# A four-layer cross-attention and expert network in two interleaved streams: a new order of the work on every engine, and one attention's mask added by VectorE

## The chip, the cores and the metric

The kernel runs on one core of a Trainium2 chip. The core has five engines that run their own instruction lists in order and wait for one another through semaphores: TensorE (PE, with its weight loads shown apart as PEld), VectorE (DVE), ScalarE (ACT), GpSimd (POOL) and SyncE (SP), which here only issues DMAs. The metric is the time on the device in microseconds (us) of one execution; lower is better.

## The reference, cut to what matters

Eight sequences of 256 rows of 128 numbers pass through four layers. Each layer adds a gated cross-attention over a fixed context and then a gated expert network:

```python
for n in range(4):
    x = x + tanh(g_xattn[n]) * attention_n(layernorm(x), ctx)
    x = x + tanh(g_ffn[n]) * experts_n(layernorm(x))

# attentions 0, 1, 2: 16 heads of 8, head by head
scores = q @ k.T * 8 ** -0.5      # 1: + adj and where(mask1 == 0, -inf)  2: where(mask0 == 0, -inf)
out = softmax(scores) @ v         # 1 and 2: then @ Wo + bo
# attention 3: one head of 64
# experts_0: gate and 8 SELU experts, best 2 weighted; experts_1: two quantised linear maps with a GELU
# experts_2: 8 experts of silu(x W1) * (x W3) W2; experts_3: 16 small experts on each of 8 heads
```

## The kernel before

The batch is cut into four turns `i` of two sequences (512 rows). Two turns run as two streams, one attention of one turn beside the expert layer of the other. `steps` writes the pairs out: step 1 is attention (0,0) alone; step 2 is attention (1,0) beside experts (0,0); 3 is (0,1) beside (1,0); 4 is (1,1) beside (0,1); 5 is (0,2) beside (1,1); 6 is (1,2) beside (0,2); 7 and 8 are the one-head attentions (0,3) and (1,3) beside experts (1,2) and (0,3); 9 is (2,0) beside (1,3); steps 10 to 16 repeat 2 to 8 with turns 2 and 3, and step 17 is experts (3,3) alone. So steps 2, 3, 10 and 11 hold a SELU layer, 4, 5, 12 and 13 the quantised ("bit") layer, 6, 7, 14 and 15 the SiLU layer, 8, 9, 16 and 17 the head experts.

Within a step, each engine's list is made by `play`: the attention and the expert layer are Python generators that `yield` a due time before each piece, and the piece with the smaller due time comes first in the list. Due times are unitless plans that decide order alone; in the run an engine takes its list in order and waits where a semaphore says so. No piece of a step comes ahead of one of the step before on the same engine.

An attention is an opening and then 36 slots. The opening: keys and values are projected on TensorE from the transposed context `cT`; VectorE normalises `x` (`statistics`, a power of -0.5 on GpSimd in `root`, `normal`); TensorE transposes it (`norm_T`) and projects the queries; VectorE splits the queries into three bf16 parts `qp` and SyncE stacks them into `qS` with 12 DMAs, while GpSimd splits the keys into `kp` and stacks them into `kS` with 12 more (`keys`). A slot is one pair of PSUM banks out of two pairs: "max" slots make scores that VectorE reduces to row maxima (L1205), "shift" slots turn the maxima round, "exp" slots make the scores again with the maxima taken off, ScalarE applies Exp (L965), and TensorE multiplies the result by the values (L587). "back" slots bring the heads back. The slots' due times start at 25 and lie 1.3 apart (`FIRST_SLOT`, `SLOT`); the SELU layer's 36 pieces of one matrix each lie 2.2 apart, the SiLU layer's 16 lie 4.2 apart. Beside expert layers 2 and 3, exp slots come in groups of four with one due time. The masks: for attention 1, GpSimd makes `b1q` (added to the max scores on TensorE through an identity, L538) and `bfull` (added to the exp scores by VectorE, `add_bias`, L1221). For attention 2, `l2_bias_k` is added to the exp scores on TensorE, L565, two matmuls a slot.

## Time and profile before

| | before |
|---|---|
| median of 3 runs | 1927.77 us (1922.35 to 1931.37) |
| the profiled execution | 1916.38 us, its span 1914.6 us |
| TensorE busy, weight loads | 1348.0 us (70%), 666.6 us |
| VectorE, ScalarE, GpSimd busy | 987.2 us (52%), 751.5 us (39%), 402.5 us (21%) |
| granted TensorE clock, mean | 0.841 of full |

The span is the stretch from the first to the last instruction of the program; the profiled execution's own time holds 1.8 us more. Engines are busy in parallel, so the shares don't add up to the span. In the windows views a row is a stretch of the span: its bounds and length, the busy us of PE, PEld, DVE, ACT and POOL with the number of instructions, the granted TensorE clock, the DMA engines' busy share and GB/s. In a timeline row the two numbers are start and length, and the brackets hold the idle time of the engine just before with what ended it. SPq is a DMA issue on SyncE. "issue" is idle time whose end the profile puts down to nothing; a wait for a DMA's landing is often shown so.

### The profile page before, as it was taken

What the parts mean: (1) busy time and instruction counts of PE and PEld (TensorE: products, weight loads), DVE (VectorE), ACT (ScalarE), POOL (GpSimd) and SP (SyncE); (2) the same over time, 40 slices, a digit from 0 to 9 for tenths busy, and PEclk for the clock granted to TensorE, in tenths of its full rate; (3) what the DMA queues carried; (4) which work ended last, traced back from release to release, by engine and by line L of the source; (5) the groups of instructions that cost most, each with busy time, mean ns of one, the idle gap of its engine ahead of it and who ended that gap; (6) DMA issues with size and microseconds to landing.
All of it is one profiled execution on the core that took longest, in us unless ns stands there. A gap on an engine that the chain in (4) does not pass through costs nothing.

```text
span 1914.6 us, 21114 instructions
## 1 busy us (share of the span) xinstructions
PE 1348.0 (70%) x7836; PEld 666.6 (35%) x7836; DVE 987.2 (52%) x2268; ACT 751.5 (39%) x1102; POOL 402.5 (21%) x462
## 2 busy tenths in 40 slices
PE   3456978865647697867477797886473869886756
PEld 2223544441212334531222455444121233453211
DVE  3347546656563453462552664666656445346252
ACT  0034643522324143337266463353232413433636
POOL 4306020025030200015332601001503020001424
PEclk9988999987559898969578898999755989896969
DMA  8204112112020200012420311300202020001221
GB/s 269 37 7 77 51 48 63 34 39 40 1 33 2 34 1 1 1 28 88 66 73 23 83 45 38 74 23 12 45 1 33 1 33 2 1 1 17 94 61 61
DMA packets 49221, 78.57 MB, mean 41 GB/s; under 512 B 15056, under 2 KB 34272, under 8 KB 48496
## 3 DMA queue, kind: packets, MB, share of 16 engines
q0 software_dynamic: 18752, 34.69, 7.7%
q1 hardware_dynamic: 25616, 25.25, 6.3%
q10 hardware_dynamic: 4752, 17.30, 2.9%
q8 instruction: 62, 1.02, 0.2%
q14 instruction: 39, 0.32, 0.1%
HBM read 52.63 MB, written 2.10 MB: 29 GB/s over the span
## 4 chain that ended last, share of the span: by engine, by line
PE 53%; DVE 18%; issue 12%; ACT 9%; DMA 4%; POOL 3%; SPq 1%; POOLq 0%; ACTq 0%; DVEq 0%
PE ps L705 5%; PE ps L587 5%; PE ps L721 5%; PE ps L538 5%; DVE nm L1205 4%; PE ps L809 4%; PE ps L863 3%; PE ps L543 3%; PE ps L811 3%; PE ps L852 3%; PE ps L799 3%; ACT hT L1075 3%; DVE ps L1221 2%; PE ps L570 2%; DVE hT L1403 1%
## 5 line engine op out<-in xcount | busy, mean ns | idle before, releaser
L341 POOL TENSOR_TENSOR rstd<-vare,mhalf 128x4 f32<-128x4 f32 x40 | 42.4, 1063 | 1191.2 <-DVE vare L1145 1131.2
L1205 DVE TENSOR_REDUCE nm<-ps 128x4 f32<-128x1024 f32 x192 | 231.8, 1222 | 113.9 <-PE ps L543 113.1
L965 ACT ACTIVATE pT<-ps 128x1024 f32<-128x1024 f32 x192 | 194.2, 1026 | 166.9 <-DVE ps L1221 103.8
L1075 ACT ACTIVATE hT<-ps,w_l_b 128x512 f32<-128x512 f32 x256 | 158.2, 684 | 91.6 <-PE ps L852 89.8
L705 PEld LDWEIGHTS ps<-l_ring,hT 128*128 128x128 f32 x1152 | 154.1, 206 | 79.7 <-issue 78.0
L705 PE MATMUL ps<-l_ring,hT 128*128 128x128 f32 x1152 | 157.8, 291 | 26.6 <-DVE acc L1343 25.1
L1403 DVE SCALAR_TENSOR_TENSOR hT<-ex,rl 128x512 f32<-128x512 f32 x144 | 104.4, 730 | 123.2 <-ACT rl L1014 99.2
L721 PE MATMUL ps<-xT,l_ring 128*128 128x512 f32 x288 | 164.9, 664 | 4.0 <-ACT rl L1014 4.0
L1013 ACT ACTIVATE ex<-ps,l_exp_bias 128x512 f32<-128x512 f32 x144 | 99.2, 689 | 172.3 <-PE ps L721 171.8
L852 PE MATMUL ps<-ex,w1s 96*128 96x512 bf16 x256 | 101.5, 438 | 75.2 <-ACT hT L1075 49.8
L587 PE MATMUL ps<-pT,vA 128*32 128x256 f32 x1536 | 122.8, 447 | 33.0 <-ACT oT L945 31.3
L1533 DVE SCALAR_TENSOR_TENSOR rl<-ps,w_l_b,gate 128x512 f32<-128x512 f32 x64 | 48.0, 751 | 158.6 <-PE ps L863 144.2
L543 PE MATMUL ps<-kS,qS 48*128 48x256 bf16 x768 | 84.0, 306 | 44.7 <-issue 27.3
L538 PE MATMUL ps<-b1q,ident_b 128*128 128x512 bf16 x256 | 75.6, 424 | 49.6 <-DMA qS<-qp 28.6
L1054 ACT ACTIVATE ex<-ps,w_l_bias 128x512 f32<-128x512 f32 x64 | 43.9, 687 | 158.7 <-PE ps L809 158.4
L570 PE MATMUL ps<-qS,kS 50*128 50x256 bf16 x768 | 83.2, 304 | 28.2 <-ACT pT L965 24.6
L499 PE MATMUL ps<-w_ident,xn 128*128 128x128 f32 x112 | 28.0, 398 | 105.3 <-DVE xn L1152 105.3
L1014 ACT ACTIVATE rl<-ps,w_l_bi 128x512 f32<-128x512 f32 x144 | 99.0, 688 | 0.0
L1464 DVE SCALAR_TENSOR_TENSOR hT<-ps,w_l_bias,ex 128x512 f32<-128x512 f32 x64 | 48.0, 749 | 94.2 <-PE ps L811 59.8
L1343 DVE SCALAR_TENSOR_TENSOR acc<-ps,gw,acc 128x128 f32<-128x128 f32 x224 | 62.9, 343 | 59.8 <-PE ps L799 35.1
L809 PE MATMUL ps<-xT,w_l_w 128*128 128x512 f32 x128 | 76.8, 684 | 18.8 <-DVE hT L1464 18.8
L1221 DVE TENSOR_TENSOR ps<-ps,bfull 128x1024 f32<-128x1024 f32 x64 | 77.2, 1227 | 21.9 <-PE ps L570 21.8
(256 smaller groups left out, 2097.7 us busy)
## 6 DMA issues: line engine op xcount, KB each, us to landing
l_ring<-in_l_wio ACTq DMA_DIRECT2D x33, 512.0 KB, 3.8
gate<-f_gate_rows POOLq DMA_DIRECT2D x64, 256.0 KB, 3.7
kS<-kp POOLq DMA_DIRECT2D x144, 64.0 KB, 3.5
qS<-qp SPq DMA_DIRECT2D x144, 64.0 KB
w_l_w<-in_l_w SPq DMA_DIRECT2D x3, 1024.0 KB
ex<-gate POOLq DMA_DIRECT2D x24, 128.0 KB, 5.3
...
```

Of the source, the lines that this page charges most:

```text
L538: pe.matmul(bank(sl + g), ident_b[:], part.rearrange("p t k -> p (t k)"), start=k == 0, stop=False, skip_group_check=True)
L543: last = pe.matmul(bank(sl + g)[:, qt * S:(qt + 1) * S], qS[row:row + KS, j, at:at + P], kS[row:row + KS, j, b * S:(b + 1) * S], start=not ...
L570: last = pe.matmul(bank(sl + g)[:, kt * S:(kt + 1) * S], kS[row:row + KX, j, at:at + P], qS[row:row + KX, j, b * S:(b + 1) * S], start=not ...
L587: last = pe.matmul(ps[32 * g:32 * g + VW, 4, w % 2 * S:(w % 2 + 1) * S], vA[:, 2 * b + kt, 2 * HP * jj + g, :], pT[:, (2 * w + g // HP) % ...
L705: last = pe.matmul(bank(7)[:, t * P:(t + 1) * P], hT[:, e % 2, fc, t * P:(t + 1) * P], wo[:, fc * P:(fc + 1) * P], start=fc == 0, stop=fc ...
L721: pe.matmul(bank(5 + n % 2), ring[:, k % RING, 0, fc * P:(fc + 1) * P], xT[s][:], start=True, stop=True).then_inc(sem("f0_in"), 1)
L809: pe.matmul(bank(5), W["l2_w1"][:, e, hc * P:(hc + 1) * P], xT[s][:], start=True, stop=True)\
L852: pe.matmul(bank(5 + n % 2), w1s[:, ep * P:(ep + 1) * P], st3[0:KS3, 4 * a + h, :], start=True, stop=True).then_inc(sem("f3_in"), 1)
L965: act.activation(pT[:, v % NPB, :], scores, ACT.Exp).then_inc(sem("p_ready"), 1)
L1075: act.activation(hid3[:, n % 8, :], bank(5 + n % 2), ACT.Gelu, bias=W["l3_b1"][:, ep:ep + 1])\
L1205: dve.tensor_reduce(nm[:, 2 * b:2 * b + 2, :, j].rearrange("p t g -> p g t"), ps[:, sl:sl + 2, :].rearrange("p g (t k) -> p g t k", t=2), ...
L1403: dve.scalar_tensor_tensor(hT[:, e % 2, fc, :], ex[:, n % 4, :], ALPHA, rl[:, n % 4, :], ALU.min, ALU.add).then_inc(sem("f0_h"), 1)
```

## The change

What it does, with the names of the new code:

- **Opening.** The normalisation and the transposes for the next attention of the same turn move from that attention's opening to the end of the expert layer before it (`next_norm`, `next_T`, and a `root` at `OVER[n] + 1`). Only attention 0, whose input comes from memory, still normalises in its opening.
- **Keys.** The next attention's keys are projected during the present attention (`keys(*after, 4)`, due 8.0, into bank 4), split on GpSimd (`key_parts`, due 23.0), and stacked into `kS` once the present attention's last exp scores are made (`key_stack`, due `end - 1`). The context's load comes earlier.
- **Pace.** Slots are due from 18.0 on, 1.3 apart, and beside the SELU layer from 27.0 on, 1.5 apart (`pace`). What follows the slots moves with them (`end_of`).
- **Masks.** `b1q` is made in `m1f`, the space of the loaded mask, and for turns 1 and 3 one step earlier; `bfull` has its space to itself.
- **Bit layer.** It is due later, and its quantisation on VectorE is cut into pieces that lie between the maxima (`quantise` yields).
- **Attention 3** is due 8.0 later than the expert layer beside it (`CLASS`).
- **Mask for the Exp in attention 2.** Where it stands beside expert layer 2 (steps 6 and 14), the two matmuls a slot on TensorE go and VectorE adds `l2_bias_k` in PSUM; in steps 5 and 13 they stay.

```diff
-FIRST_SLOT, SLOT = 25.0, 1.3
+def pace(layer):
+    return (27.0, 1.5) if layer == 0 else (18.0, 1.3)
...
-END = FIRST_SLOT + 36 * SLOT
+def end_of(layer):
+    first, slot = pace(layer)
+    return first + 36 * slot
+CLASS = 8.0
...
+            def key_parts(m):
+                if m:
+                    pool.wait_ge(sem("k_stack"), 16 * HP * NSEG * m)
                 pool.wait_ge(*upto("kf", m, 1))
...
+            def key_stack(m):
+                pool.wait_ge(*upto("kp", m, 1))
                 if m:
                     pool.wait_ge(*upto("s2", m - 1, 2 * NK))
...
+                if after is not None:
+                    yield 23.0
+                    key_parts(place(*after))
...
+                if a == 1 and i % 2 == 0:
+                    yield 34.0
+                    bias(i + 1, 0)
+                    yield end - 12.0
+                    query_bias(i + 1)
+                    mask_in(i + 1, 1)
+                if after is not None:
+                    yield end - 1.0
+                    key_stack(place(*after))
+                yield end + 8.0
                 root(i)
...
+                if a == 0:
+                    yield 6.0
+                    norm_T(i, LN_OF_ATT[a])
+                    yield 7.5
+                pe.wait_ge(*of("xT_ready", i, 7, n_T(LN_OF_ATT[a])))
+                pe.matmul(bank(3), W[L + "wq"][:], xT[s][:], start=True, stop=True).then_inc(sem("q_ps"), 1)
...
+                if after is not None:
+                    yield 8.0
+                    keys(*after, 4)
...
-                    bias = [l2_bias_k[:]] if a == 2 else []
+                    bias = [l2_bias_k[:]] if a == 2 and beside(i, a) != 2 else []
...
+                yield OVER[0] + 3.0
+                next_T(i, 0)
...
+                    own = bfull[:, 2 * b:2 * b + 2, :] if a == 1 else l2_bias_k[:]
+                    full = own.unsqueeze(1).to_broadcast([P, HP, 2, S])
+                    dve.tensor_tensor(both, both, full, ALU.add).then_inc(sem("biased" if a == 1 else "masked"), 1)
...
+            def next_norm(i, n):
+                statistics(i, x[i % 2])
+                yield OVER[n] + 2.0
+                normal(i, x[i % 2])
...
+BIT_ROOTS = (0.5, 22.0)
+OVER = (SLOT_0 * (N0 + 8), 47.0, SLOT_2 * (N2 + 3) + 10.0)
```

Line numbers differ between the two kernels. On TensorE before, where step 3 gives way to step 4: the last products of the SELU layer, the gate's transposes and its bias, the keys and values, then `norm_T`, the bit layer's transposes, the queries and the bit layer's first map, and the first slot's mask and scores.

```order
L705 MATMUL ps<-l_ring,hT 128x128 x28
L732 MATMUL ps<-w_ident,gw 8x128 x4
L737 MATMUL ps<-l_exp_bo,y 128x128 x4
L520 MATMUL ps<-cT,w_l_wk 128x512
L522 MATMUL ps<-w_l_wv,cT 128x128 x4
L499 MATMUL ps<-w_ident,xn 128x128 x4
L749 MATMUL ps<-ident_b,gates 128x128 x4
L529 MATMUL ps<-xT,w_l_wq 128x512
L757 MATMUL ps<-w1q,gates 128x512 x4
L538 MATMUL ps<-b1q,ident_b 128x512 x4
L543 MATMUL ps<-kS,qS 128x256 x4
```

On TensorE of the changed kernel, the same place:

```order
L771 MATMUL ps<-l_ring,hT 128x128 x8
L798 MATMUL ps<-w_ident,gw 8x128 x4
L803 MATMUL ps<-l_exp_bo,y 128x128 x4
L537 MATMUL ps<-w_ident,xn 128x128 x4
L571 MATMUL ps<-xT,w_l_wq 128x512
L573 MATMUL ps<-w_l_wv,cT 128x128 x4
L555 MATMUL ps<-cT,w_l_wk 128x512
L817 MATMUL ps<-ident_b,gates 128x128 x4
L825 MATMUL ps<-w1q,gates 128x512 x4
L587 MATMUL ps<-b1q,ident_b 128x512 x4
L592 MATMUL ps<-kS,qS 128x256 x4
```

The keys, first in their step before, are now those of the next attention and stand behind the queries; the transposes of `xn` stand ahead of the step.

On VectorE before, in the opening of step 4: the bit layer's first quantisation up to its result `gates`, the attention's values `vA`, its normal form `xn`, and the first of the query parts `qp`:

```order
L1350 TENSOR_SCALAR vare<-cols 128x4
L1353 TENSOR_TENSOR cols<-cols,rstd 128x4
L1354 TENSOR_SCALAR cols<-cols 128x4
L1355 RECIPROCAL cols<-cols 128x4
L1356 SCALAR_TENSOR_TENSOR cols<-cols,rstd 128x4
L1357 TENSOR_SCALAR cols<-cols,wmean 128x4
L1360 TENSOR_SCALAR xn<-xn,cols 128x128 x4
L1363 TENSOR_SCALAR xn<-xn 128x512
L1364 TENSOR_SCALAR gates<-xn 128x512
L1185 TENSOR_TENSOR vA<-ps,w_l_bv 128x64x8
L1152 TENSOR_SCALAR xn<-x,mv,rstd 128x128 x4
L1196 CAST qp<-attT 128x512
```

On VectorE of the changed kernel, the same opening:

```order
L1236 TENSOR_SCALAR vare<-mv 128x4
L1243 TENSOR_SCALAR xn<-x,mv,rstd 128x128 x4
L1518 TENSOR_TENSOR y<-xn 128x512
L1519 TENSOR_REDUCE cols<-xn 128x4
L1520 TENSOR_REDUCE cols<-y 128x4
L1441 TENSOR_SCALAR vare<-cols 128x4
L1275 CAST qp<-attT 128x512
L1276 TENSOR_TENSOR oT<-attT,qp 128x512
L1277 CAST qp<-oT 128x512
L1278 TENSOR_TENSOR qp<-oT,qp 128x512
L1286 TENSOR_TENSOR vA<-ps,w_l_bv 128x64x8
L1445 TENSOR_TENSOR cols<-cols,rstd 128x4
```

The query parts moved from behind the bit layer's first quantisation to ahead of it (from L1445 on), and the normal form of `x` stands first.

On VectorE of the changed kernel in step 6, in the second half of the slots (L1567 the SiLU layer's product, L1434 its weighted sum, L1313 the mask, which has no counterpart in the list before):

```order
L1313 TENSOR_TENSOR ps<-ps,l_bias_k 128x1024 x4
L1567 SCALAR_TENSOR_TENSOR hT<-ps,w_l_bias,ex 128x512
L1313 TENSOR_TENSOR ps<-ps,l_bias_k 128x1024 x3
L1318 COPY oT<-ps 128x2x256
L1313 TENSOR_TENSOR ps<-ps,l_bias_k 128x1024
L1567 SCALAR_TENSOR_TENSOR hT<-ps,w_l_bias,ex 128x512
L1434 SCALAR_TENSOR_TENSOR acc<-ps,gw,acc 128x128 x4
L1567 SCALAR_TENSOR_TENSOR hT<-ps,w_l_bias,ex 128x512
```

Up to four mask additions now stand in a row between two pieces of the SiLU layer.

## Rows read from the trace of the kernel before

**Rows 1.** Busy time by window, steps 2 to 6, then steps 10 to 16 (us)
```profile
140.50:270.50 130.00, 104.39 (x668) 65.29 (x668) 73.86 (x140) 65.20 (x98) 30.81 (x28) 0.91 0.24 58
270.50:416.90 146.40, 118.37 (x742) 68.65 (x740) 88.94 (x167) 64.08 (x97) 13.83 (x19) 0.93 0.18 48
416.90:530.30 113.40, 64.69 (x409) 26.29 (x408) 70.92 (x100) 30.87 (x43) 32.95 (x29) 0.66 0.12 21
530.30:629.50 99.20, 55.83 (x412) 21.91 (x413) 54.75 (x118) 31.06 (x44) 15.95 (x22) 0.78 0.11 17
629.50:751.50 122.00, 100.43 (x584) 50.15 (x585) 56.31 (x132) 42.27 (x51) 12.80 (x19) 0.91 0.09 14
...
1054.70:1829.60 774.90, 575.67 (x3346) 294.99 (x3346) 418.50 (x924) 305.26 (x450) 142.34 (x157) 0.84 0.13 31
```

**Rows 2.** The same view, openings of steps 2, 4, 5, 6, 10; sum over eleven
```profile
140.50:177.00 36.50, 23.90 (x90) 13.87 (x92) 21.95 (x42) 16.95 (x28) 23.25 (x24) 0.83 0.50 86
...
416.90:455.20 38.30, 9.24 (x29) 4.01 (x28) 25.63 (x51) 8.82 (x17) 30.84 (x28) 0.63 0.36 59
530.30:567.40 37.10, 10.12 (x28) 4.83 (x28) 24.86 (x63) 8.64 (x17) 14.54 (x20) 0.55 0.27 43
629.50:662.80 33.30, 24.13 (x82) 13.45 (x82) 13.71 (x46) 7.29 (x11) 10.88 (x17) 0.86 0.31 48
...
1054.70:1087.70 33.00, 24.44 (x90) 14.12 (x91) 18.27 (x40) 18.24 (x29) 20.01 (x23) 0.84 0.36 85
...
sum 395.00, PE 197.26 PEld 105.19 DVE 228.26 ACT 129.00 POOL 196.97; mean PE 17.93 PEld 9.56 DVE 20.75 ACT 11.73 POOL 17.91
```

**Rows 3.** Timeline of the opening of step 4: start us, us, engine, line
```profile
417.10 0.75 DVE L1159 SCALAR_TENSOR_TENSOR x<-ps,tg,x 128x512 f32<-128x512 f32 x1 [0.42 <-PE ps L737]
...
421.56 1.98 POOL L341 TENSOR_TENSOR rstd<-vare,mhalf 128x4 f32<-128x4 f32 x2 [14.60 <-DVE vare L1350]
...
428.24 1.10 DVE L1152 TENSOR_SCALAR xn<-x,mv,rstd 128x128 f32<-128x128 f32 x4
...
431.26 2.07 PE L529 MATMUL ps<-xT,w_l_wq 128*128 128x512 f32 x2 [0.26 <-ACT xT L907]
...
437.17 7.90 SPq L1589 DMA_DIRECT2D qS<-qp  x12
...
453.42 1.87 PE L538 MATMUL ps<-b1q,ident_b 128*128 128x512 bf16 x4 [14.29 <-DMA qS<-qp]
```

**Rows 4.** Timeline of the opening of step 5
```profile
552.49 7.89 SPq L1589 DMA_DIRECT2D qS<-qp  x12
...
566.45 1.01 PE L538 MATMUL ps<-l_bias_q,ident_b 128*128 128x512 bf16 x2 [12.01 <-issue]
```

**Rows 5.** Busy time by window: inside the slots of step 4 and of step 3
```profile
486.00:529.00 43.00, 30.66 (x218) 13.14 (x215) 20.91 (x24) 15.95 (x18) 0.00 (x0) 0.53 0.00 1
...
310.00:400.00 90.00, 78.95 (x546) 42.63 (x545) 58.91 (x86) 44.25 (x66) 0.00 (x0) 0.96 0.11 36
```

**Rows 6.** Groups by line and form: busy us, mean ns, idle us before
```profile
L721 PE MATMUL ps<-xT,l_ring 128*128 128x512 f32 x288 | 164.9, 664 | 4.0 <-ACT rl L1014 4.0
...
L705 PE MATMUL ps<-l_ring,hT 128*128 128x128 f32 x1152 | 157.8, 291 | 26.6 <-DVE acc L1343 25.1 <-DVE acc L1341 0.8 <-DVE y L1374 0.4
...
L1221 DVE TENSOR_TENSOR ps<-ps,bfull 128x1024 f32<-128x1024 f32 x64 | 77.2, 1227 | 21.9 <-PE ps L570 21.8
...
L565 PE MATMUL ps<-l_bias_k,ident_b 128*128 128x512 bf16 x128 | 40.7, 401 | 5.9 <-DMA qS<-nmT 3.0 <-ACT pT L965 2.3 <-DVE att L1235 0.6
```

**Rows 7.** Timeline of step 2, GpSimd mask work beside VectorE
```profile
163.34 4.00 POOL L353 TENSOR_SCALAR bfull<-m 128x1024 f32<-128x1024 int32 x1 [4.53 <-DMA m<-in_mask_q]
...
165.45 0.69 DVE L1403 SCALAR_TENSOR_TENSOR hT<-ex,rl 128x512 f32<-128x512 f32 x1 [1.62 <-PE ps L705]
...
182.43 1.27 DVE L1403 SCALAR_TENSOR_TENSOR hT<-ex,rl 128x512 f32<-128x512 f32 x1 [1.56 <-PE ps L705]
```

**Rows 8.** Timeline of GpSimd in the opening of step 9
```profile
934.98 3.17 POOL L434 DMA_DIRECT2D ex<-gate  x6
```

356 lines of the change are left out of this document (204 added, 152 removed).

## The prediction

> **What bounds the kernel now.** I read the span as 17 steps and first asked the windows view how busy the engines are in each [rows 1]. No engine is busy throughout: TensorE is the busiest, with 104.4 of 130.0 us in step 2, 118.4 of 146.4 in step 3 and 100.4 of 122.0 in step 6, but 64.7 of 113.4 in step 4 and 55.8 of 99.2 in step 5. Steps 10 to 16 are one row of 774.9 us, the first seven measured again. So each step is bound partly by TensorE's work and partly by waits, and the second question is where in a step the waits lie.
>
> The same view over the openings alone, from the first projection to the first scores, gives it [rows 2]: the eleven openings last 395.0 us, and TensorE is busy for 197.3 of them, by half. In the bit layer's steps it is busy for 9.2 of 38.3 us (step 4) and 10.1 of 37.1 (step 5). Once the slots run in step 3, TensorE is busy for 78.95 of 90 us, 88% [rows 5]; there the work itself sets the pace. The timeline of the opening of step 4 shows the chain that is waited for [rows 3]: the SELU layer's result is added to x until 417.85; the normal form of x begins only at 428.24, behind the bit layer's quantisation on the same engine; the queries are projected from 431.26; the DMAs that stack their parts are issued from 437.17; the first mask matmul starts at 453.42. Of these 35.6 us 10.4 lie ahead of the normal form, 8.9 between it and the first DMA, and 16.25 in the stacking. In step 5 the stacking takes 13.96 us, 552.49 to 566.45 [rows 4].
>
> **The change part by part.** I give each step a term, negative where it saves.
>
> *Steps 4 and 12.* The chain starts from the SELU layer's end as before, but nothing stands in it that isn't its own. Statistics take about 1.5 us, the root 1.0 (two took 1.98 in [rows 3]), the normal form 1.1, transposes and copy about 1.9, the queries 2.1 [rows 3], their copy and parts some 3.8, and the hops between seven engines' pieces an estimated 1: 12.4 in place of 19.3, so 7 less. The stacking is now alone on the DMA engines, since the keys' 12 DMAs went out in the step before: 14.0 in place of 16.25 [rows 3, 4], 2.3 less. The opening saves 9. Against that, the second quantisation, which lay in the opening and cost the attention nothing there, now lies between the maxima: VectorE is busy 70.9 of 113.4 us in step 4 and 25.6 of the 38.3 of its opening [rows 1, 2], and about 12 us of that move under the slots. If half of it isn't hidden, 6 come back. I take 3 as the rest of the saving at this place, and another 3 from the masks and key parts that no longer stand on GpSimd ahead of the bit layer's root: -6 each. Bounds: 0 and -13.
>
> *Steps 5 and 13.* The attention's input is done in the middle of the step before, so the queries can be projected at once. From the step's start at 530.3 to the DMAs were 22.2 us [rows 1, 4]; projection 2.1, copy 0.7, parts 3.1 and, on VectorE ahead of them, the other stream's statistics and the bit layer's first reductions (about 4 us) leave some 8: -14. The same quantisation under the slots gives 4 back: -10 each. Bounds: -4 and -15.
>
> *Steps 2 and 10, 3 and 11 (SELU).* Here the opening isn't idle: 23.9 of 36.5 us busy [rows 2]. The order puts 13 pieces of the SELU layer ahead of the first slot in place of 12, and one piece costs (164.9 + 157.8) / 144 = 2.24 us of TensorE [rows 6]. The opening then holds 23.9 + 2.2 = 26.1 us of work; the chain of attention 0 (normalisation, queries, stacking) needs some 27. I take 29 to 30 us, so -7 in step 2; the rest of the step has one piece less (-2), and its tail, where TensorE waited for the normal form with SELU work still behind it, is better filled (-3): -12. In step 10 the opening was shorter by 3.5 already (33.0 us [rows 2]), so -8. In steps 3 and 11 the opening, much like step 2's, gets some 7 shorter by the same sum, the tail gains 4, and the new chain at the end of step 2, x to transposed x, costs 5 in which TensorE has nothing left to do: -6 each. Bounds for a SELU step: the idle time of its opening, 12.6 [rows 2], and nothing.
>
> *Steps 6 and 14.* The opening saves some 7 of its 33.3, since 24.1 of them are TensorE's work [rows 2]. Of attention 2's 128 mask matmuls 64 go, 64 x 0.401 = 25.7 us of TensorE, and 32 additions at 1.227 = 39.3 us come to VectorE [rows 6]. VectorE has room (56.3 of 122.0 busy [rows 1]), so the sum of work isn't the question. A group of four exp slots is: per slot two matmuls (0.8) go from the chain and an addition (1.23) and a hop come in, +0.6 a slot where TensorE waits in the group, and four additions, 4.9 us, stand before the SiLU layer's next product. I take +2 in all for the mask: -5 each. Bounds: +8 and -12.
>
> *Steps 7, 8, 15, 16.* The SiLU layer now ends with the norm chain (+5), but the one-head attention no longer stands ahead of the head experts' first matmul (-5); the keys' 12 DMA issues come between GpSimd's sums of the head experts (7 us of issue, two sums of slack). I take 0.
>
> *Steps 9 and 1.* In step 9 GpSimd issued the head experts' stacking DMAs only at 934.98 [rows 8], behind the keys' 12, whose issue takes about 7 us. These are now issued a step earlier, as is the load they shared the DMA engines with: -9, the bounds 0 and -12. In step 1 the chain is the old one: 0.
>
> Sum: -12 -6 -6 -10 -5 -9 = -48 in the first half, -8 -6 -6 -10 -5 = -35 in the second, together -83. From the profiled execution's 1916.4 us this gives 1833. The median of the three runs shown stands 11 above the profiled execution; with it the same sum gives 1845. I predict 1840, between them.
>
> *A shared port.* In [rows 7] the GpSimd mask operation of 4.00 us lies over a VectorE product at its usual 0.69, and another product beside mask work took 1.27: beside GpSimd a VectorE operation loses nothing or 0.6. The change moves two of the four mask preparations (some 17 us each) from a bit opening to a SELU step with a product every 3 to 4 us, about five products each: 2 x 5 x 0.6 = 6 us of VectorE time at most, and VectorE isn't the bound there, so it has no term. The Trainium skill, "SBUF — State Buffer", section "SBUF: two separate sides", has it that GpSimd and a VectorE operation with two SBUF inputs take the shared ports in turn, for the whole instruction. By that rule the product at 165.45 would have waited until 167.34, and the trace disagrees there; with a wait of 2 us for each of the ten products the sum would be 20 us less good, 1860.
>
> **The rivals.**
>
> *A, the gain is larger, through the clock.* In the second half of step 4's slots TensorE was granted 0.53 of its clock, near the lower of its two levels (1.2 of 2.4 GHz), and was busy for 30.7 of 43 us [rows 5], after an opening with 9 us of work in 38 [rows 2]. If a shorter idle opening keeps the full clock there, half of 30.7, or 15 us, goes from its busy time; if 10 of it is on the path, in four steps, -40 more: 1800. The trace speaks half for it: step 5 had the same opening and 0.78 over the step [rows 1]. The Trainium skill, "TensorE: Matmul & The Clock Gate", says in "HAM oscillation — how this bites in real kernels" that idle gaps bring the lower clock, which would speak for this rival.
>
> *B, most is given back.* The openings shrink as forecast, but the work that lay in them (VectorE 228 us over the eleven [rows 2]) lengthens the slots by nearly as much, since the slots are a chain of two bank pairs rather than a stretch of one engine's work. With two thirds of the 83 lost: -28, 1900.
>
> *C, slower: the SELU steps go by the slots, not by TensorE's work.* From first scores to the addition to x, step 3 took 305.6 to 417.85, 112 us, and I have 103 to 105 for it. If the 36 slots are really paced by their due distance, 1.5 in place of 1.3 makes about 96 us of slots into 111, +15, and the norm chain's 5 stands behind it. Four such steps, +20 each in place of -32 together, make -83 into +29: 1945 in the profile's terms. It decides from 21 us lost in each of the four, when that stretch reaches 124 us. Against it: due times order a list and hold nobody up, and TensorE was 88% busy there [rows 5]. For it: the 12% are waits of just this chain.
>
> *D, no difference.* The due times merely trade places among waits: idle time in the openings turns up in the slots. It would need B's loss to be whole: 1916.
>
> **How the numbers follow.** My forecast (1790 to 1870) 0.64, A 0.12, B 0.11, D 0.05, C 0.08. The range is to hold 8 in 10: 1785 to 1895 has the forecast, most of A's upper part and a part of B. A difference under 0.5% (10 us) can hardly be told from none in this kernel. Faster by more than that: 0.64 + 0.12 + 0.11 = 0.87; the same 0.06, slower 0.07, with C and D split so.
>
> **What would show it.** Right: openings from first projection to first scores of about 22 to 24 us in steps 5 and 13, 28 to 31 beside SELU, with no "issue" wait ahead of the first mask matmul there; the key stack's DMAs issued before the step's end; SELU steps at 90% TensorE busy or more; the mask additions at 1.23 us with steps 6 and 14 no longer than 118. Wrong: a stretch of 120 us or more from first scores to the addition to x in step 3; gaps of VectorE's maxima behind the GELU or the root in steps 4 and 5; a root on GpSimd waiting behind the keys' stacking; SiLU pieces over 6 us apart in the exp groups.

## The result, and the profile after

The changed kernel takes 1904.39 us (median of 4 runs, 1902.7 to 1908.52) against 1929.57 us for the kernel before on the same chip (4 runs, 1922.35 to 1938.3): ratio 0.9871, 95% interval 0.9826 to 0.9916. The direction was right and the size was not: some 25 us gained, 83 forecast, and 1904 lies outside the range of 1785 to 1895. The profiled execution took 1902.7 us, its span 1900.7 us. That of the kernel before took 1916.38 us, 13 us less than the median of its four runs: it was a quick one, which matters for the table below.

From the page of the changed kernel: busy time by engine, the granted clock in 40 slices, and two groups with telling idle time.

```profile
PE 1354.7 (71%) x7772; PEld 667.1 (35%) x7772; DVE 1026.9 (54%) x2300; ACT 756.9 (40%) x1106; POOL 398.1 (21%) x462
...
PEclk9669989877658887978679998998785998895959
...
L1047 ACT ACTIVATE pT<-ps 128x1024 f32<-128x1024 f32 x192 | 195.2, 1027 | 159.5 <-DVE ps L1313 113.9
...
L787 PE MATMUL ps<-xT,l_ring 128*128 128x512 f32 x288 | 163.7, 658 | 18.7 <-DMA l_ring<-in_l_wio 10.7
```

TensorE's busy time hardly moved (1348.0 to 1354.7 us), although 64 mask matmuls are gone; the mean granted clock is 0.826 where it was 0.841. These are single executions: in 53 others, of 1915 to 1936 us, the kernel before went from 0.817 to 0.849, and in eight the changed kernel went from 0.812 to 0.833. VectorE has 39.7 us more, about the 32 mask additions. The SELU layer's first matmuls wait 10.7 us for weights, where before they waited 4.0 us in all, for ScalarE [rows 6]. The wait before the Exp looks large, but it was there before, in the same group of the kernel before:

```profile
L965 ACT ACTIVATE pT<-ps 128x1024 f32<-128x1024 f32 x192 | 194.2, 1026 | 166.9 <-DVE ps L1221 103.8
```

The Exps wait 159.5 us where they waited 166.9; the part put down to additions on VectorE, those of attention 1 included, rose from 103.8 to 113.9. Sums over the whole span don't show what the new additions cost. The steps do.

The windows view of the changed kernel, for openings and whole steps. A step here runs from the last addition to x (L1250) of the step before to its own last one; its opening ends at the first scores. In order: opening of 3, step 3, opening of 4, step 4, opening of 5, step 5, opening of 6, step 6, step 8.

```profile
262.20:296.10 33.90, 25.85 (x110) 15.73 (x110) 20.43 (x52) 17.67 (x29) 12.80 (x9) 0.90 0.33 55
262.20:416.20 154.00, 124.27 (x740) 73.22 (x740) 92.80 (x168) 64.20 (x97) 25.71 (x26) 0.90 0.20 49
416.20:444.60 28.40, 10.15 (x30) 4.39 (x30) 15.01 (x37) 8.84 (x17) 8.57 (x5) 0.56 0.21 28
416.20:525.30 109.10, 68.12 (x413) 27.41 (x413) 70.86 (x113) 31.16 (x44) 20.91 (x23) 0.66 0.10 15
525.30:548.50 23.20, 9.30 (x24) 3.71 (x26) 12.74 (x37) 8.15 (x16) 2.15 (x2) 0.57 0.26 34
525.30:614.40 89.10, 60.55 (x408) 21.91 (x408) 50.05 (x96) 30.35 (x43) 14.40 (x20) 0.73 0.12 19
614.40:645.50 31.10, 17.95 (x65) 9.72 (x66) 12.06 (x49) 6.12 (x9) 1.04 (x1) 0.83 0.20 26
614.40:744.20 129.80, 94.81 (x550) 50.00 (x550) 74.57 (x149) 43.32 (x51) 2.05 (x2) 0.87 0.05 7
822.10:924.40 102.30, 69.31 (x280) 25.30 (x280) 43.19 (x167) 52.20 (x86) 43.43 (x55) 0.76 0.24 62
```

Cut at the same events, all 17 steps, in us. "After" is the mean of two profiled executions of the changed kernel, this one and e1; they differ by up to 3.6 us in a step. "Miss" is what was measured less what was forecast.

| step | 1 | 2 | 3 | 4 | 5 | 6 | 7 | 8 | 9 |
|---|---|---|---|---|---|---|---|---|---|
| before | 133.0 | 138.4 | 146.4 | 112.4 | 93.5 | 124.4 | 74.3 | 92.1 | 138.7 |
| after | 134.5 | 127.2 | 152.3 | 108.7 | 88.5 | 130.1 | 78.0 | 103.4 | 130.5 |
| forecast | 0 | -12 | -6 | -6 | -10 | -5 | 0 | 0 | -9 |
| miss | +1.4 | +0.8 | +11.9 | +2.3 | +5.0 | +10.7 | +3.7 | +11.3 | +0.7 |

| step | 10 | 11 | 12 | 13 | 14 | 15 | 16 | 17 |
|---|---|---|---|---|---|---|---|---|
| before | 132.0 | 146.7 | 113.1 | 93.3 | 124.4 | 75.9 | 92.5 | 80.6 |
| after | 118.7 | 150.5 | 106.6 | 88.6 | 128.5 | 77.1 | 95.5 | 82.8 |
| forecast | -8 | -6 | -6 | -10 | -5 | 0 | 0 | 0 |
| miss | -5.2 | +9.8 | -0.5 | +5.2 | +9.1 | +1.2 | +3.0 | +2.2 |

The misses add up to 73 us. By the medians the miss is 58 (83 forecast, 25 measured); the other 15 come mostly from the quick execution that the row "before" shows. 42 of the 73 lie in four steps, 3 and 11 and 6 and 14, which got longer where they were to get shorter; 11 lie in step 8.

The chain that the forecast began with, in the timeline of the changed kernel: the opening of step 4, then of step 5 (compare [rows 3, 4]).

```profile
415.38 0.75 DVE L1250 SCALAR_TENSOR_TENSOR x<-ps,tg,x 128x512 f32<-128x512 f32 x1
...
418.78 1.11 DVE L1243 TENSOR_SCALAR xn<-x,mv,rstd 128x128 f32<-128x128 f32 x4 [1.12 <-POOL rstd L358]
...
428.81 7.90 SPq L1697 DMA_DIRECT2D qS<-qp  x12
...
442.79 1.86 PE L587 MATMUL ps<-b1q,ident_b 128*128 128x512 bf16 x4 [6.08 <-DMA qS<-qp]
...
533.54 7.90 SPq L1697 DMA_DIRECT2D qS<-qp  x12
...
547.53 1.01 PE L587 MATMUL ps<-l_bias_q,ident_b 128*128 128x512 bf16 x2 [6.56 <-issue]
```

From the end of the addition (416.13) to the normal form 2.65 us where there were 10.4, on to the first DMA 10.0, and 14.0 in the stacking. The opening of step 4 went from 37.4 to 28.5 us and that of step 5 from 37.1 to 23.2: the forecast 9 and 14. The gain is there; it was given back elsewhere.

### The profile page after: what moved, and what is told of

The parts are those of the page before. It is cut to its first block, busy times and chain, and to the rows that moved or that the text cites. A ratio compares the mean times of both kernels' runs of the same rounds, so it can differ in the third digit from the quotient of the medians.

```text
span 1900.7 us, 21058 instructions
## 1 busy us (share of the span) xinstructions
PE 1354.7 (71%) x7772; PEld 667.1 (35%) x7772; DVE 1026.9 (54%) x2300; ACT 756.9 (40%) x1106; POOL 398.1 (21%) x462
## 4 chain that ended last, share of the span: by engine, by line
PE 49%; DVE 24%; issue 9%; ACT 8%; DMA 5%; POOL 3%; SPq 1%; ACTq 0%; POOLq 0%; DVEq 0%
PE ps L771 6%; DVE nm L1296 5%; PE ps L638 5%; PE ps L787 4%; PE ps L587 4%; PE ps L879 3%; PE ps L869 3%; DVE ps L1313 3%; PE ps L935 3%; PE ps L924 3%; PE ps L881 3%; PE ps L592 2%; ACT hT L1166 2%; DVE acc L1434 2%; PE ps L619 2%
## 5 line engine op out<-in xcount | busy, mean ns | idle before, releaser
L1296 DVE TENSOR_REDUCE nm<-ps 128x4 f32<-128x1024 f32 x192 | 231.0, 1221 | 128.8 <-PE ps L592 128.0
L1047 ACT ACTIVATE pT<-ps 128x1024 f32<-128x1024 f32 x192 | 195.2, 1027 | 159.5 <-DVE ps L1313 113.9
L1504 DVE SCALAR_TENSOR_TENSOR hT<-ex,rl 128x512 f32<-128x512 f32 x144 | 108.7, 765 | 130.3 <-ACT rl L1099 114.2
L787 PE MATMUL ps<-xT,l_ring 128*128 128x512 f32 x288 | 163.7, 658 | 18.7 <-DMA l_ring<-in_l_wio 10.7
L405 POOL DMA_DIRECT2D kS<-kp x144 | 81.2, 572 | 323.9 <-PE ps L619 323.6
L592 PE MATMUL ps<-kS,qS 48*128 48x256 bf16 x768 | 88.0, 317 | 28.4 <-issue 17.1
L935 PE MATMUL ps<-hT,w_l_w 128*32 128x512 f32 x512 | 79.5, 696 | 16.9 <-DVE rl L1637 14.3
L537 PE MATMUL ps<-w_ident,xn 128*128 128x128 f32 x112 | 28.1, 399 | 87.2 <-DVE xn L1243 87.2
L1313 DVE TENSOR_TENSOR ps<-ps,bfull 128x1024 f32<-128x1024 f32 x64 | 77.5, 1226 | 17.4 <-PE ps L619 17.3
```

The costliest lines, as they stand in the source:

```text
L592: last = pe.matmul(bank(sl + g)[:, qt * S:(qt + 1) * S], qS[row:row + KS, j, at:at + P], kS[row:row + KS, j, b * S:(b + 1) * S], start=not ...
L787: pe.matmul(bank(5 + n % 2), ring[:, k % RING, 0, fc * P:(fc + 1) * P], xT[s][:], start=True, stop=True).then_inc(sem("f0_in"), 1)
L935: last = pe.matmul(ps[32 * h:32 * h + 32, 7, :], W["l3_w2"][:, k % NEP, :], hid3[:, (4 * k + h) % 8, :], start=True, stop=True)
L1047: act.activation(pT[:, v % NPB, :], scores, ACT.Exp).then_inc(sem("p_ready"), 1)
L1296: dve.tensor_reduce(nm[:, 2 * b:2 * b + 2, :, j].rearrange("p t g -> p g t"), ps[:, sl:sl + 2, :].rearrange("p g (t k) -> p g t k", t=2), ...
L1313: dve.tensor_tensor(both, both, full, ALU.add).then_inc(sem("biased" if a == 1 else "masked"), 1)
```

## The experiments

Times are medians. The kernel before, on the same chip, took 1931.68 us (e1 to e4), 1925.94 (e5 to e8), 1925.19 (e9 to e11), 1925.98 (e12), 1925.94 (e13, e14); these differ by up to 6.5 us, so times from different groups are compared no closer than that. Times of single steps come from one profiled execution of each run.

| run | median us | ratio to before, 95% interval |
|---|---|---|
| e1 changed kernel again | 1907.49 | 0.9869 [0.9809, 0.9929] |
| e2 mask by TensorE in steps 6, 14 | 1889.04 | 0.9792 [0.9752, 0.9832] |
| e3 before, mask by VectorE in steps 6, 14 | 1950.86 | 1.0101 [1.0069, 1.0133] |
| e4 SELU pace 25.0 / 1.3 | 1893.27 | 0.98 [0.9766, 0.9834] |
| e5 key stack early in step 8 | 1914.82 | 0.9942 [0.991, 0.9973] |
| e6 `CLASS` 0 | 1909.16 | 0.9933 [0.9885, 0.998] |
| e7 part of the quantisation left out | 1893.02 | 0.9836 [0.9773, 0.9899] |
| e8 e2 and e4 together | 1875.24 | 0.9745 [0.9695, 0.9794] |
| e9 e8, keys late in step 8 | 1863.69 | 0.9683 [0.9648, 0.9719] |
| e10 mask by VectorE in 5, 13 too | 1934.92 | 1.0072 [1.0038, 1.0107] |
| e11 e8, bit pace 25.0 / 1.3 | 1873.69 | 0.9745 [0.9692, 0.9799] |
| e12 e9, quantisation in one piece | 1878.07 | 0.975 [0.9717, 0.9783] |
| e13 e9, GpSimd reads less | 1854.69 | 0.9635 [0.9609, 0.9661] |
| e14 e9 again | 1865.78 | 0.969 [0.9664, 0.9716] |

### The mask addition: e1, e2, e3, e10

> The changed kernel once more, as the measure for the runs beside it. It had 1904 us, 0.987 of before. Every theory expects 1900 to 1908 and the same steps: 6 and 14 at 130 and 128 us, 5 and 13 at 89 and 88, 2 and 10 at 126 and 119.

> The changed kernel with attention 2's mask for the Exp back on TensorE in steps 6 and 14 (two matmuls a slot in place of VectorE's addition); nothing else. Theory M (the mask addition made the chain of an exp group longer): a group of four took about 7.5 us with the addition and should take some 5.5 without, four groups, so steps 6 and 14 get 8 us shorter each, 1888. Rival W (these steps got longer only because the SiLU layer's pieces and the key work now lie under the slots, whoever adds the mask): within 4 us of the changed kernel, 1900 to 1908, since TensorE takes back 12.8 us of work in each of the steps.

```diff
-                    bias = [l2_bias_k[:]] if a == 2 and beside(i, a) != 2 else []
+                    bias = [l2_bias_k[:]] if a == 2 else []
```

> The kernel before with only one part of the change: in steps 6 and 14 VectorE adds attention 2's mask for the Exp. Theory M: slower than before by the same 8 us a step, 1943 against 1928. Rival W: the same as before within 5 us; or a gain, if TensorE's 25.7 us of mask matmuls were on the path, down to 1915.

```diff
-                    bias = [l2_bias_k[:]] if a == 2 else []
+                    bias = [l2_bias_k[:]] if a == 2 and not i % 2 == 1 else []
...
+                        elif a == 2 and i % 2:
+                            add_bias(sl, n)
```

Against e1, e2 has step 6 at 119.6 in place of 130.5 us and step 14 at 119.1 in place of 129.5; the whole is 18.5 us less. Put into the kernel before, the same edit takes both steps from 124.4 to 135.1 and 135.0, and the whole up by 19.2. So the edit costs about 10.5 us a step (10.4 to 10.9), in the old order and in the new.

The timeline of the changed kernel shows where, in one group of four exp slots of step 6:

```profile
692.31 0.61 PE L619 MATMUL ps<-qS,kS 50*128 50x256 bf16 x8
692.75 2.36 DVE L1313 TENSOR_TENSOR ps<-ps,l_bias_k 128x1024 f32<-128x1024 f32 x2 [1.66 <-PE ps L619]
...
694.01 2.15 ACT L1047 ACTIVATE pT<-ps 128x1024 f32<-128x1024 f32 x2 [0.47 <-DVE ps L1313]
...
695.09 0.39 PE L619 MATMUL ps<-qS,kS 50*128 50x256 bf16 x4 [1.17 <-ACT pT L1047]
...
696.79 1.02 ACT L1047 ACTIVATE pT<-ps 128x1024 f32<-128x1024 f32 x1 [0.62 <-DVE ps L1313]
...
697.80 0.74 DVE L1567 SCALAR_TENSOR_TENSOR hT<-ps,w_l_bias,ex 128x512 f32<-128x512 f32 x1
...
698.19 1.03 ACT L1047 ACTIVATE pT<-ps 128x1024 f32<-128x1024 f32 x1
```

The same group with the mask on TensorE (e2, timeline):

```profile
684.17 1.28 ACT L1045 ACT_TABLE_LOAD   x1
...
684.65 0.39 PE L619 MATMUL ps<-qS,kS 50*128 50x256 bf16 x4
...
685.46 1.94 ACT L1045 ACTIVATE pT<-ps 128x1024 f32<-128x1024 f32 x2
...
687.81 1.02 ACT L1045 ACTIVATE pT<-ps 128x1024 f32<-128x1024 f32 x1 [0.41 <-PE ps L619]
...
689.20 1.03 ACT L1045 ACTIVATE pT<-ps 128x1024 f32<-128x1024 f32 x1
```

From the first scores to the last Exp's end it is 6.91 us with VectorE and 5.58 with TensorE. A table load stands ahead of the first Exp in both (with VectorE at 692.26, for 1.28 us). With VectorE the first Exp starts 1.7 us after its scores, and the SiLU product L1567 stands behind all four additions. In e2's group the first slot's 0.6 us of mask was hidden, since the table load ahead of the first Exp ended only at 685.45; in the other three groups of the step the first Exp starts 0.43 us after its scores, so there the first slot's mask was not. Over all four groups of step 6, from a group's first matmul, the mask's included, to its last Exp's end, it is 28.3 us with VectorE and 23.0 with TensorE. That makes 5.3 of the 10.5.

Two things can make the other half, and no run took them apart. The SiLU layer's products come later behind the additions. And TensorE was granted a lower clock: step 6 in the windows view of e2, to be compared with the row of step 6 above (94.81 us, x550, 0.87):

```profile
609.10:728.70 119.60, 95.98 (x582) 48.55 (x582) 55.96 (x132) 42.74 (x51) 2.04 (x2) 0.93 0.05 8
```

TensorE is busy nearly as long without the mask's 32 matmuls as with them: the other 550 took it 88.7 us in e2 and 94.8 in the changed kernel. In the old order it is the same, 92.2 us at 0.90 before and 98.0 at 0.84 in e3. How much of these 6 us is on the path isn't known, nor what lowers the clock.

> The changed kernel, with the mask of attention 2 also added by VectorE in steps 5 and 13, where the exp slots stand alone and not in groups of four. 64 mask matmuls of 0.4 us leave TensorE, 32 additions of 1.23 us come to VectorE. Theory G (what costs 10.5 us in steps 6 and 14 is the chain inside a group of four slots, matmuls, addition, Exp, one after another on two bank pairs): ungrouped slots hide it better, and steps 5 and 13 grow by 0-4 us, the whole 1904-1912. Theory V (it is VectorE's own time, 39 us in two steps, where VectorE stands on the path beside the quantisation): steps 5 and 13 grow by 8-14 each, the whole 1922-1932. Against both: TensorE's 12.8 us a step less would shorten them, the whole under 1900.

```diff
-                    bias = [l2_bias_k[:]] if a == 2 and beside(i, a) != 2 else []
+                    bias = []
```

Steps 5 and 13, where exp slots stand alone, go from 89.2 and 87.8 to 98.8 and 100.3. The price is 10 to 12 us without groups too, so grouping isn't its cause: theory V. Here too the granted clock went down, from 0.73 and 0.76 to 0.67 and 0.60, and the price holds what that costs. An addition puts VectorE, 1.23 us, between scores and Exp, and the same engine makes the maxima that the other slots wait for.

### The pace beside the SELU layer: e4, e8

> The changed kernel with the slots beside the SELU layer due from 25.0 on and 1.3 apart, as before, in place of 27.0 and 1.5. Theory P (the wider pace stretched the slots of steps 3 and 11, which are 8 and 1 us longer from first scores to the addition to x): steps 3 and 11 get 5 to 8 us shorter, 1890. Rival T (TensorE's work and the norm chain at the end set these steps, not the pace): steps 2, 3, 10 and 11 stay within 3 us, or get longer by up to 5 each, since the attention ends earlier and SELU pieces are left without cover ahead of the norm chain: 1904 to 1920.

```diff
-    return (27.0, 1.5) if layer == 0 else (18.0, 1.3)
+    return {0: (25.0, 1.3)}.get(layer, (18.0, 1.3))
```

Steps 3 and 11 go from 150.5 and 152.2 (e1) to 143.2 and 143.2; steps 2 and 10 get 2 us longer each; the whole is 14.2 less. Of the 7.3 and 9.0 us, 4.7 and 3.0 lie in the openings (34.8 to 30.1, 34.2 to 31.2), which have one SELU piece less, and the rest behind them. The end of step 3 in the timelines, first the changed kernel and then e4; the `oT` row adds the attention, the `ps` row ends the SELU layer.

```profile
408.97 0.75 DVE L1250 SCALAR_TENSOR_TENSOR x<-oT,tg,x 128x512 f32<-128x512 f32 x1
...
415.38 0.75 DVE L1250 SCALAR_TENSOR_TENSOR x<-ps,tg,x 128x512 f32<-128x512 f32 x1
```

```profile
392.81 0.75 DVE L1250 SCALAR_TENSOR_TENSOR x<-oT,tg,x 128x512 f32<-128x512 f32 x1
...
407.68 0.75 DVE L1250 SCALAR_TENSOR_TENSOR x<-ps,tg,x 128x512 f32<-128x512 f32 x1 [0.42 <-PE ps L803]
```

With a distance of 1.5 the attention ends 6.4 us ahead of the layer, and what follows it has little SELU work left to lie beside; with 1.3 it ends 14.9 us ahead. e4 changed the first due time and the distance together; which of the two does how much isn't shown.

> The changed kernel with both edits at once: attention 2's mask for the Exp on TensorE, and the slots beside the SELU layer due from 25.0 on, 1.3 apart. If the two costs are separate places, they add: 18 and 14 us less than the changed kernel, 1872 to 1876. If they overlap (one wait stood in for the other), 1885 to 1890.

Its edit is those of e2 and e4 together. The steps show that the two gains add: 3 and 11 took 143.5 and 142.6 us, as in e4, and 6 and 14 took 119.3 and 120.4, as in e2. The whole, 1875.24, agrees with 18.5 and 14.2 taken from e1 (1874.8), but more closely than can be relied on: the kernel before was 5.7 us quicker on e8's chip than on e1's.

### The quantisation under the slots: e7, e11, e12

> The changed kernel without three operations of the bit layer's second quantisation: its row maximum over 2048 numbers (2.3 us), the scaling in four parts (1.7) and the clipping (1.2). Theory Q (under the slots this work is not hidden at all, since VectorE's maxima are back to back there): each of steps 4, 5, 12 and 13 gets 5.2 us shorter, 1883. Rival H (half of it hides behind waits for scores): 2 to 3 us each, 1894.

```diff
+                if n == 0:
                     for t in range(NT):
                         ins = dve.tensor_scalar(src[:, t, :], src[:, t, :], cols[:, 5, t:t + 1], -128.0,
...
-                step(dve.tensor_reduce(cols[:, 1, :], hh[:], AX.X, ALU.max, apply_absolute_value=True))
```

5.2 us of VectorE a step are gone (2.28, 1.67 and 1.22). From first scores to the end, steps 4, 5, 12 and 13 take 71.9, 59.3, 70.9 and 59.9 us; e2, whose bit steps are those of the changed kernel, has 76.3, 64.6, 76.7 and 65.7. That is 4.4 to 5.8 less: these three operations are hardly hidden at this place. The steps speak for theory Q, the whole doesn't: e7 is 32.9 us under its kernel before and e1 24.2 under its own, 8.7 apart, where theory Q had 21 and rival H 10. Steps that the edit doesn't touch differ from run to run by several us, so the steps themselves are the better measure, but they are single executions. The clock helps in part too: in e7 it was 0.82 in steps 5 and 13, in e2 0.76 and 0.73. Beside e5, where step 13 had 0.79, the gain there is 4.2 us. Two windows of the changed kernel in step 5, from the first scores on:

```profile
548.50:558.50 10.00, 7.29 (x35) 1.38 (x34) 8.92 (x11) 0.00 (x0) 3.88 (x5) 0.67 0.01 2
558.50:568.50 10.00, 6.28 (x28) 1.15 (x26) 9.83 (x14) 0.00 (x0) 0.63 (x1) 0.50 0.00 0
```

VectorE is busy for 9.83 of 10 us. That it is busy for 50.05 of the step's 89.10 us doesn't tell this: the work lies where the maxima are densest.

> The kernel of e8 with the slots beside the bit layer due from 25.0 on, as they were before the change, in place of 18.0. Theory Q (the second quantisation's work on VectorE costs what it takes wherever it lies once the openings are short): steps 4, 5, 12, 13 change by under 2 us each and the whole is 1872-1882. Rival: with later slots the quantisation comes ahead of the first maxima, the slots behind it run undisturbed as before the change (rest of step 5 56.4 in place of 65), while the opening grows by less: 3-5 us gained a step, the whole 1858-1866. Other rival: the opening grows by what the quantisation takes and the slots give back nothing: +5 a step, the whole 1890-1898.

```diff
-    return {0: (25.0, 1.3)}.get(layer, (18.0, 1.3))
+    return {0: (25.0, 1.3), 1: (25.0, 1.3)}.get(layer, (18.0, 1.3))
```

The whole stays within 2 us of e8. Steps 4 and 12 are 3 to 4 us longer, more than the 2 that theory Q allowed, step 6 is 2.7 shorter and step 8 is 3.8: within this noise the work moves and doesn't go.

> The kernel of e9 with the second quantisation of the bit layer in one piece on VectorE again (the gap between its parts 0 in place of 2.6), where its first part stood; nothing else moves. Theory Q (VectorE's time is what it costs, since VectorE has no idle time at this place, however the work is cut): steps 4, 5, 12, 13 stay at 104-107 and 87-91, the whole 1860-1868. Rival 1: the cut is what costs, since each part makes the maxima's bank pairs wait in turn; in one piece the steps get 2-4 us shorter, the whole 1850-1857. Rival 2: the cut is what hides part of it, and in one piece, with the root's wait in the middle, each step gets 2-4 us longer, the whole 1870-1880.

```diff
-                yield from quantise(i, hh[:], qh, F0, 1, 20.0, 2.6, "f1_qh")
+                yield from quantise(i, hh[:], qh, F0, 1, 20.0, 0.0, "f1_qh")
```

14.4 us slower than e9. Steps 4, 5, 12 and 13 take 108.9, 91.3, 109.0 and 91.2 in place of 105.2, 89.0, 104.3 and 87.2. Rival 2 holds: cutting the work into pieces hides 2 to 5 us of it a step, and theory Q as stated is false. The clock isn't the reason, since it was no lower in three of e12's four steps (0.74, 0.77, 0.74, 0.77 against 0.69, 0.73, 0.77, 0.77) and the fourth lost as much. VectorE's timeline in step 4 of e12 shows what the piece leaves behind it:

```profile
450.48 2.35 DVE L1298 TENSOR_REDUCE nm<-ps 128x4 f32<-128x1024 f32 x2
454.23 1.23 DVE L1298 TENSOR_REDUCE nm<-ps 128x4 f32<-128x1024 f32 x1 [1.40 <-PE ps L596]
456.32 2.52 DVE L1298 TENSOR_REDUCE nm<-ps 128x4 f32<-128x1024 f32 x2 [0.86 <-PE ps L596]
```

TensorE stood still for 10.8 us until 451.76, since both bank pairs were full while VectorE worked at the piece, and VectorE waits for new scores afterwards.

### Keys among the head experts: e5, e6, e9

> The changed kernel with one thing moved: in steps 8 and 16, GpSimd stacks the next attention's keys right behind their split, ahead of the head experts' gate rows, and not amid their sums. (Step 16 has no next attention, so only step 8 can change.) Theory K (the 12 issues, 6.7 us amid the sums, are what made step 8 longer, 102 to 104 us against 92 before): step 8 falls to 96 to 98 us. Rival L (step 8 is long because the one-head attention is due 8.0 later and shares the stretch of the gate multiplications): step 8 stays at 102 or grows by up to 7, since the issues now stand ahead of the gate rows.

```diff
+                    if a == 3:
+                        key_stack(place(*after))
...
-                if after is not None:
+                if after is not None and a < 3:
                     yield end - 1.0
                     key_stack(place(*after))
```

> The changed kernel with the one-head attention due from 0.0 as before and not from 8.0 (CLASS). Theory L: steps 7, 8, 15 and 16, which are 3 to 10 us longer than before, fall by 3 to 5 each, 1890. Rival K: steps 8 and 16 stay within 2 us; 1904.

```diff
-CLASS = 8.0
+CLASS = 0.0
```

e5 issues the key stack of step 8 ahead of the head experts' gate rows; step 8 takes 109.5 us, more than the 102.3 and 104.5 of the changed kernel's two profiles, so theory K as it stood there, with its 96 to 98, failed: earlier is worse. e6 sets `CLASS` to 0: step 8 takes 100.0, but steps 15 and 16 take 82.6 and 100.6 in place of 77.9 and 95.3 (e1), and the whole is no better. So the 8.0 isn't what made step 8 longer, or only a few us of it.

> The kernel of e8 with one thing moved: in step 8 the split of the next attention's keys (key_parts) and their stacking (key_stack) are due 80, behind GpSimd's sums of the head experts, in place of 23 and end - 1. Theory K: step 8 is longer than before (107.0 in e8 against 92.1, and 95.5 in step 16, which has no next keys) because this key work stands on GpSimd ahead of the gate rows' DMA and between the sums. Then step 8 falls to 96-100, step 9 takes back at most 3, and the whole gives 1862-1870 us. Rival: the work only trades places, the stacking comes late for the scores of step 9, whose opening (27-28 us now) goes back to 34-36, and the whole stays at 1875 within 5. Second rival: step 8 is long because of the keys' projection on TensorE and its copy, not because of GpSimd; then step 8 stays at 105-107 and the whole is 1875-1885.

```diff
+                if after is not None and a == 3:
+                    yield 80.0
+                    key_parts(place(*after))
+                    key_stack(place(*after))
```

(`key_parts` at 23.0 and `key_stack` at `end - 1.0` are kept for the attentions 0 to 2.) Step 8 goes from 107.0 to 99.4, and the opening of step 9 takes back 2.1 (26.4 to 28.5). The 7.6 us are against e8's step 8, the longest of its kind. In the eight profiles that have this key work in step 8 where the changed kernel has it, the step took 102.3 to 107.0 us, 104.2 in the mean; in the four that have it late (e9, e12, e13, e14) 97.9 to 99.4, mean 98.6. So the place of the key work is worth 5.7 us. This is the best version with all its work: 1863.69, and 1865.78 when repeated (e14). GpSimd's timeline in e8:

```profile
881.38 1.29 POOL L492 TENSOR_TENSOR rl<-rl 128x512 f32<-128x512 f32 x1
882.60 6.70 POOL L405 DMA_DIRECT2D kS<-kp  x12
889.30 0.60 POOL L456 DMA_DIRECT2D gate<-f_gate_rows  x1
889.92 4.11 POOL L492 TENSOR_TENSOR rl<-rl 128x512 f32<-128x512 f32 x3
```

and in e9:

```profile
891.18 1.26 POOL L496 TENSOR_TENSOR rl<-rl 128x512 f32<-128x512 f32 x1 [1.33 <-DVE rl L1637]
892.38 0.61 POOL L392 CAST kp<-kf 128x512 bf16<-128x512 f32 x1
...
896.43 6.73 POOL L405 DMA_DIRECT2D kS<-kp  x12 [0.30 <-POOL kp L395]
```

In e8 the 12 issues hold GpSimd for 6.70 us; a gate row and three sums come out behind them in a row. The forecast's "two sums of slack" was too little.

### GpSimd and VectorE at once: e13, e14

> The kernel of e9 with part of the arithmetic left out: the second and third bf16 part of the keys and the second part of the query mask are filled with zeros (memset) in place of being computed, so GpSimd has no subtraction and no second copy there (24 subtractions and 12 copies on the keys, 4 and 4 on the masks). In e9 86 VectorE instructions lie over GpSimd compute and take over 0.06 us more than the same instruction alone, 45 us in all; about 20 of it stands beside just these GpSimd instructions (VectorE's L1449, 0.23 us alone, takes 1.206 beside a subtraction of 1.15). Theory S (the two share a port, and VectorE waits until GpSimd's instruction that reads SBUF has ended): the excess falls from 45 to 25-30 us, SELU products L1504 and the bit layer's small columns go back to 0.69 and 0.23, and the time falls by 3-12 us against e14, as far as the excess is on the path. Rival T (VectorE is slower at these places for another reason, such as waiting for its own semaphores): the excess stays over 40. Rival U (the excess goes, but all of it lay in VectorE's idle time): the excess falls and the time stays within 3 us of e14.

> The kernel of e9 once more, beside e13 on the same chip: 1860-1868 us, VectorE's excess beside GpSimd 45-48 us.

```diff
-                step(pool.tensor_tensor(kf[:], kf[:], kp[:, 0, :], ALU.subtract))
-                step(pool.tensor_copy(kp[:, 1, :], kf[:]))
-                pool.tensor_tensor(kp[:, 2, :], kf[:], kp[:, 1, :], ALU.subtract).then_inc(sem("kp"), 1)
+                step(pool.memset(kp[:, 1, :], 0.0))
+                pool.memset(kp[:, 2, :], 0.0).then_inc(sem("kp"), 1)
...
-                step(pool.tensor_tensor(m1f[:], m1f[:], b1q[:, 0], ALU.subtract))
-                step(pool.tensor_copy(b1q[:, 1], m1f[:]))
+                step(pool.memset(b1q[:, 1], 0.0))
```

One instruction shows the effect, a VectorE operation on 128x4 elements in the bit layer. Its durations (ns, least, median, most) in e14 and, as L1447, in e13:

```profile
L1449 DVE TENSOR_SCALAR cols<-cols,wmean x8: 229/717/1206, 419.3 to 1427.4; 128x4 f32<-128x4 f32 x8
```

```profile
L1447 DVE TENSOR_SCALAR cols<-cols,wmean x8: 229/229/230, 414.7 to 1418.5; 128x4 f32<-128x4 f32 x8
```

I added up, over all VectorE instructions that lie over GpSimd compute, what each takes beyond the median of the same instruction alone, where that is over 0.06 us: 31.0 us in 48 instructions before the change, 47.7 in 90 after it, 46.3 in 86 in e14 and 21.5 in 42 in e13. (Instructions of one line are taken together; with their shapes kept apart it is 29.9, 43.6, 42.2 and 20.1 us.) With 24.8 us of it gone the kernel is 11.1 us faster (1865.78 to 1854.69), 3 us of that in each of steps 3 and 11. Theory S holds in its main part: the excess went and the time with it. GpSimd also has less to do in e13, which can't be separated from this. And a fill isn't free for every VectorE operation: beside one, L1444 of e13 (128x4 elements, one tensor read) took 0.52 to 0.55 us in place of 0.17.

## Why the prediction was right in sign and wrong in size

- **Openings of the bit and SiLU steps: right.** Those of steps 4, 5 and 9 got 9, 14 and 14 us shorter, that of step 6 got 8. Step 9 as a whole (-8 for -9) and steps 2 and 10 (-11 and -13 for -12 and -8) came out as forecast or better.
- **Openings beside SELU: wrong in steps 3 and 11.** The forecast had "some 7 shorter by the same sum" and 28 to 31 us: measured 34.0 and 34.2, no less than before (34.2 and 33.4). In step 3 TensorE has the work forecast (25.85 us for 26.1), but 8 us of waits beside it, for `xn` 4.7, for a weight load 1.9, for ScalarE the rest. Its last part is set by the 13 pieces in the list and not by the stacking, whose DMAs went out at 276.72, 19 us ahead of the first scores. With e4's pace it is 30 to 31.
- **The term of the mask: the failed step. "I take +2 in all for the mask": measured +10.5 in each step** (e2, e3). By the forecast's own price, +0.6 a slot, the 16 exp slots of a step would have cost 9.6 us if TensorE waited in all of them. It took 2, with "VectorE has room" as the reason, so it counted the rest as hidden. VectorE's share of the step told nothing about this: the addition stands between the scores and the Exp, on the engine that also makes the maxima and the SiLU layer's products, while part of the mask matmuls had lain under the table load or an Exp. The groups alone got 5.3 us longer; the other half is the later SiLU products or the lower clock, or both, and stays open. 8.5 us a step, 17 in all: the largest mis-sized term.
- **Rival C, half of it.** Its place and mechanism were right (the SELU steps lengthen by the slots' distance), its price too high: the stretch from first scores to the addition in step 3 was 120 us in this profile (116 in e1) and 115 in step 11 (118), against the 124 at which it was to decide. Step 3 stood just at the forecast's own sign of being wrong, 120 us. "Due times order a list and hold nobody up" is true and was no argument: the order decides which engine runs out of work at the step's end. The pace's share is 14 us in all (e4), and part of it lies in the openings.
- **"If half of it isn't hidden, 6 come back" and "gives 4 back".** Steps 4 and 12 came out at -3.7 and -6.5 against -6. In steps 5 and 13 the slots grew by 8 to 9.5 us in place of 4, where VectorE is busy for 9.83 of 10 us; 10 us in the two steps. e7 took out three of the moved operations and shows it for them; for the rest of the growth it is argued.
- **Step 8 at 0: measured +11.** The place of the key work on GpSimd is 5.7 of it (e9 and the profiles beside it). The other 5 the old order shows too. e3 leaves everything but steps 6 and 14 as before, and its steps 8 and 16 took 97.1 and 97.8 us where the other profile of the old order has 92.1 and 92.5:

```profile
835.70:932.80 97.10, 69.72 (x281) 24.80 (x282) 41.06 (x172) 51.43 (x84) 33.52 (x40) 0.74 0.21 57
1767.40:1865.20 97.80, 69.74 (x278) 24.98 (x278) 41.08 (x172) 51.33 (x84) 33.57 (x40) 0.73 0.21 54
```

TensorE was busy for 69.7 us at a clock of 0.74, against 63.84 at 0.80. Steps 1 and 17 went from 133.0 and 80.6 to 137.2 and 85.6 in the same way, so the misses there and in step 16 (1.4, 2.2 and 3.0) are no larger than what two executions of one order differ by. Steps 7 and 15 took 4 and 1 us more than forecast; e3 has 74.3 in both, as the kernel before has in step 7. Their cause isn't settled.
- **Rival A, the clock: in part.** From before to this profile the granted clock stayed at 0.66 in step 4, rose from 0.65 to 0.74 in step 12, and fell from 0.78 to 0.73 in step 5 and from 0.79 to 0.76 in step 13. Steps 4 and 12 do the same work; at 0.66 TensorE was busy for 68.1 us and the step took 109.1, at 0.74 it was 62.8 and 104.9. In e2, e4 and e6 it was step 4 that had 0.74 to 0.77, and took 105.0, 104.4 and 103.4 us. So behind a shorter opening the clock was sometimes higher, for 4 to 6 us a step and not A's 10, and in steps 5 and 13 it was lower. In step 16 the same matmuls cost TensorE more time than in the first profile: the windows of steps 8 and 16 before, and then of step 16 after.

```profile
822.50:914.60 92.10, 63.84 (x278) 23.77 (x278) 41.09 (x172) 51.14 (x84) 33.60 (x40) 0.80 0.22 61
1738.80:1831.30 92.50, 64.85 (x278) 23.51 (x278) 40.95 (x172) 51.15 (x84) 33.63 (x40) 0.79 0.21 57
```

```profile
1718.50:1814.30 95.80, 68.22 (x274) 23.82 (x274) 42.46 (x167) 51.18 (x84) 33.44 (x39) 0.73 0.21 55
```

TensorE's busy time rises from 64.85 to 68.22 us with no more instructions, at a clock of 0.73 where it was 0.79: 3.4 us, as much as the step grew, and less than e3's 4.9 in the old order. What lowers the clock isn't known.

- **The shared port: "it has no term" was wrong.** The forecast rested on the one product at 165.45 that ran at 0.69 under a 4.00 us operation [rows 7]. That product began 2.1 us after the operation; products that began sooner after one did wait: at 1092.14 of the same trace one began 0.3 us after such an operation and took 1.52. The excess rose by 16.7 us of VectorE time (13.7 with the shapes kept apart); at e13's rate (11.1 of 24.8 on the path) this is an estimated 7 us of the 73, spread over the steps and in part within the terms above. The 20 us of waits that the forecast got by the rule of the Trainium skill, "SBUF — State Buffer", section "SBUF: two separate sides", were close to these 16.7 as VectorE time, and too much as time on the path.

Counted together: the mask 17, the pace 14, the second quantisation in steps 5 and 13 10, the keys in step 8 6. That is 47 of the 73 us with an experiment or a row behind each. Some 12 more, in steps 1, 8, 16 and 17, are no more than the old order's own two profiles differ by, with the clock. The rest, 14 us, is in the SELU openings and in steps 7 and 15, as far as it isn't the port's. Rival B's time, 1900, and its loss of two thirds came nearest, but that was luck for the most part: in steps 6 and 14 nothing that lay in an opening came back, new work did, and in steps 3 and 11 it was the order.
